# Two 16-head attentions in one Trainium2 program: two heads side by side in the row halves of TensorE

## The reference

```
# l1a, causal with a slope per head
scores = einsum('bhqd,bhkd->bhqk', q, k) * 8**-0.5
bias   = -slopes[h] * (pos[q] - pos[k])            # slopes[h] = 2**(-0.5 * (h + 1))
scores = where(pos[q] >= pos[k], scores + bias, -inf)
out    = (softmax(scores) @ v) @ Wo.T
# l3b, each block of 128 queries sees its own and the two neighbouring blocks of keys
scores = einsum('bhnqd,bhnkd->bhnqk', q, k_ctx) * 8**-0.5
scores = where(abs(q_pos - k_pos) <= 128, scores, -inf)
out    = (softmax(scores) @ v) @ Wo.T + bo
```

## Time and profile before

| what | value |
|---|---|
| median of 3 runs | 3575.45 us (3564.14 to 3583.17) |
| profiled execution, its own time | 3585.18 us |
| its span | 3583.1 us |
| PE busy over the span | 2880.5 us (80%) |
| DVE busy over the span | 1859.3 us (52%) |
| causal call: norm and projections, attention | 1195 to 1252, 1252 to 1564 us |
| windowed call: norm and projections, attention | 3189 to 3233, 3233 to 3475 us |

### The profile page before, as it was taken

How to read it: one execution, slowest core, us unless ns; L and a number is a source line. 1 busy time by engine, 2 the same in 40 slices (tenths; PEclk the granted TensorE clock), 3 DMA queues, 4 the chain that set the end, 5 groups by cost and what they waited for, 6 DMA issues and landing times. The chain is left out here.

```text
span 3583.1 us, 54951 instructions
## 1 busy us (share of the span) xinstructions
PE 2880.5 (80%) x21418; PEld 1480.1 (41%) x21486; DVE 1859.3 (52%) x3533; ACT 1405.9 (39%) x2681; POOL 765.2 (21%) x632
## 2 busy tenths in 40 slices
PE   6565878778888498989768888998888877768986
PEld 3454247423357234434322222342332434555555
DVE  5311245478964388711378888203763543536733
ACT  3211424432234246642356777422221222234652
POOL 1000006245617201000443340003530001230003
PEclk9666869878889789989879999997998989878987
DMA  2022001121101422100031010000510001023302
GB/s 109 15 63 74 0 12 45 37 72 65 53 20 51 112 44 37 21 1 0 14 70 28 12 24 1 0 0 17 145 49 0 0 1 48 20 71 62 51 6 70
DMA packets 86479, 136.40 MB, mean 38 GB/s; under 512 B 13319, under 2 KB 52199, under 8 KB 84947
## 3 DMA queue, kind: packets, MB, share of 16 engines
q1 hardware_dynamic: 79187, 118.50, 13.1%
q0 software_dynamic: 7040, 14.43, 1.5%
HBM read 106.81 MB, written 25.85 MB: 37 GB/s over the span
## 5 line engine op out<-in xcount | busy, mean ns | idle before, releaser
L1655 ACT ACTIVATE at_pt<-PS 128x384 f32<-128x384 f32 (+3 forms) x704 | 288.5, 455 | 237.7 <-PE PS L1567 202.5
L1705 DVE TENSOR_REDUCE at_mp<-PS 128x1 f32<-128x384 f32 (+3 forms) x640 | 313.5, 538 | 115.1 <-PE PS L1555 98.9
L1552 PE MATMUL PS<-at_kx,at_qx 72*128 72x384 bf16 (+5 forms) x640 | 219.0, 347 | 66.8 <-DMA at_kx<-L_attn_a_parts 26.8
L1565 PE MATMUL PS<-at_qx,at_kx 105*128 105x512 bf16 (+5 forms) x704 | 214.4, 314 | 7.8 <-ACT at_pt L1655 5.9
L4300 DVE CUSTOM_DVE_ANT_0 PS<-PS,ls_pt 128x1024 f32<-128x1024 f32 x128 | 153.8, 1237 | 19.1 <-ACT ls_pt L4153 15.5
L4153 ACT ACTIVATE ls_pt<-PS,ls_far 128x512 f32<-128x512 f32 x256 | 155.5, 686 | 18.6 <-PE PS L3974 10.1
L2425 DVE TENSOR_TENSOR_SCAN mb_ring<-PS,mb_ring 128x1024 f32<-128x1024 f32 x64 | 146.6, 2291 | 19.4 <-POOL mb_ring L2364 6.7
L2380 PE MATMUL PS<-mb_ring,ident 128*128 128x512 f32 x256 | 147.2, 728 | 6.0 <-DVE mb_ring L2430 6.0
L1227 DVE SCALAR_TENSOR_TENSOR X<-PS,small_L,X 128x512 f32<-128x512 f32 x8 | 6.0, 751 | 261.2 <-PE PS L1175 261.2
L2409 ACT ACTIVATE PS<-mb_dt,mb_a 128x1024 f32<-128x1024 f32 x64 | 71.5, 1118 | 174.8 <-DVE mb_ring L2425 169.5
L1578 PE MATMUL PS<-at_pt,at_v 128*9 128x256 f32 (+3 forms) x1408 | 130.7, 451 | 5.5 <-issue 1.4
(11 more groups left out here) (825 smaller groups left out, 6557.2 us busy)
## 6 DMA issues: line engine op xcount, KB each, us to landing
rw_arena<-rw_v_rows SPq DMA_DIRECT2D x32, 512.0 KB, 4.6
dl_arena<-in_fir_bank SPq DMA_DIRECT2D x32, 256.0 KB, 3.1
lnA<-mb_rows SPq DMA_DIRECT2D x16, 512.0 KB, 3.7
XN<-mb_rows SPq DMA_DIRECT2D x16, 512.0 KB, 3.7
ffn_place<-in_ffn_L SPq DMA_DIRECT2D x4, 1152.0 KB, 16.7
at_qx<-L_attn_a_parts SPq DMA_DIRECT2D x24, 192.0 KB
at_kx<-L_attn_a_parts SPq DMA_DIRECT2D x72, 64.0 KB
at_qx<-L_attn_b_parts SPq DMA_DIRECT2D x24, 192.0 KB
```

What stands on the lines that cost most here:

```text
L1552: mm = nc.tensor.matmul(PS[:, n % 3, 0:e - c], QX[0:RAW, u % 3, g, blk(i, P)], KX[0:RAW, u % 3, g, c:e], start=True, stop=True)
L1565: mm = nc.tensor.matmul(PS[:, 3 + n % 3, 0:e - c], KX[0:FULL, u % 3, g, blk(j, P)], QX[0:FULL, u % 3, g, c:e], start=True, stop=True)
L1655: nc.scalar.activation(PT[:, y % SLOTS, g, 0:e - c], PS[:, 3 + n % 3, 0:e - c], ACT.Exp, scale=SCALE).then_inc(exp_done, 1)
L1705: nc.vector.tensor_reduce(best, sc, AX.X, ALU.max).then_inc(s_maxed, 1)
```

## The change

- **Row halves.** A head takes 48 rows of products (six pairs of parts in place of nine), six slope rows (causal) and three rows of maxima: 57 or 51 rows. Two of the four heads stand in rows 0 to 63 (lane 0), two in rows 64 to 127 (lane 1). The first pass takes heads 0, 2, 1, 3 (lanes 0, 1, 0, 1), the second 2, 0, 3, 1 (lanes 1, 0, 1, 0), so that neighbours on PE stand in different lanes. DVE and ACT follow these orders.
- **Masks inside the halves.** `mask` adds one tile with two products of 64 rows in the head's own lane: `identb` with ABOVE, and EYE2 with OTHER (the identity and the mask of the other half). One covers 128 columns and the other 64. They are issued after both passes' products: score, turned score, score's masks, turned score's masks.
- **Loads.** 22 DMAs (causal) or 18 (windowed) per unit, with half as many elements per part; before 12 (13 for the first three units of the causal call).
- **Slopes.** POOL makes the whole slope table beside the norm, and `load` copies the rows by DMA. The work of DVE and ACT on them, L1494 and the copies of L1670 are gone, as are the two fills of 32 rows. The fixed rows of KX come from PHI, PLO and UNIT by six DMAs (windowed: two) after the stores of m = 0.
- **First load.** `load(0)` is issued after the stores of m = 3, and those of m = 4 to 7 follow it.
- `lower` sends its rows with two DMAs in place of one.

```diff
-    MROW = 102 if causal else 72
-    RAW, FULL = (102, 105) if causal else (72, 75)
...
+    LANES, SPLIT = 2, ((0, 0), (0, 1), (0, 2), (1, 0), (1, 1), (2, 0))
+    SLOPES = 6 if causal else 0
+    PLACE = 8 * len(SPLIT)
+    RAW = PLACE + SLOPES
+    FULL = RAW + 3
+    EACH = HG // LANES
+    LOADS = LANES * (9 + (EACH if causal else 0))
+    lane_rows = lambda lane, n: slice(64 * lane, 64 * lane + n)
+    head_first = lambda t: 2 * (t % 2) + t // 2
+    head_second = lambda t: 2 * (1 - t % 2) + t // 2
...
-        QX, KX = sb("at_qx", [P, 3, HG, SEQ], BF16), sb("at_kx", [P, 3, HG, SEQ], BF16)
+        QX, KX = sb("at_qx", [P, 3, HG // LANES, SEQ], BF16), sb("at_kx", [P, 3, HG // LANES, SEQ], BF16)
...
+        ABOVE, OTHER, EYE2 = sb("at_above", [P, 2, P], BF16), sb("at_other", [P, 2, P], BF16), sb("at_eye2", [P, P], BF16)
...
-            SLT = sb("at_slt", [P, 16])
-            KROWS = sb("at_krows", [P, SEQ], BF16)
...
         def load(sp, u):
-            heads, tokens = slice(HG * (u % 4), HG * (u % 4) + HG), blk(u // 4, SEQ)
-            for n in range(3):
-                rows = slice(24 * n, 24 * n + 24)
-                sp.dma_start(QX[rows, u % 3, :, :], parts[0, heads, :, :, tokens].rearrange("g c d t -> (c d) g t")).then_inc(LOADED[u % 3], 16)
-                if causal and n == 0 and u < 3:
-                    sp.dma_start(KX[72:96, u, :, :], parts[1, heads, :, :, tokens].rearrange("g c d t -> (c d) g t")).then_inc(LOADED[u], 16)
-                for c in range(3):
-                    rows = slice(24 * n + 8 * c, 24 * n + 8 * c + 8)
-                    sp.dma_start(KX[rows, u % 3, :, :], parts[1, heads, n, :, tokens].rearrange("g d t -> d g t")).then_inc(LOADED[u % 3], 16)
+            tokens = blk(u // 4, SEQ)
+            for lane in range(LANES):
+                heads = slice(HG * (u % 4) + EACH * lane, HG * (u % 4) + EACH * lane + EACH)
+                top = 64 * lane
+                for p, (c, _) in enumerate(SPLIT):
+                    sp.dma_start(QX[top + 8 * p:top + 8 * p + 8, u % 3, :, :], parts[0, heads, c, :, tokens].rearrange("g d t -> d g t")).then_inc(LOADED[u % 3], 16)
+                for at, n in ((0, 3), (24, 2), (40, 1)):
+                    sp.dma_start(KX[top + at:top + at + 8 * n, u % 3, :, :], parts[1, heads, 0:n, :, tokens].rearrange("g c d t -> (c d) g t")).then_inc(LOADED[u % 3], 16)
+                if causal:
+                    for g in range(EACH):
+                        slopes = SLT[0:SLOPES, heads.start + g, :].unsqueeze(1).to_broadcast([SLOPES, 8, SEQ // 8])
+                        sp.dma_start(QX[top + PLACE:top + RAW, u % 3, g, :].rearrange("p (r t) -> p r t", r=8), slopes).then_inc(LOADED[u % 3], 16)
...
+                own(pool.tensor_copy(EYE2[:, 0:64], k.identb[:, 64:P]))
+                own(pool.tensor_copy(EYE2[:, 64:P], k.identb[:, 0:64]))
+                for n in range(2):
+                    sign = 2 * n - 1
+                    own(pool.memset(OTHER[:, n, :], 0.0))
+                    own(pool.memset(TURN[:, :], 0.0))
+                    own(pool.affine_select(out=OTHER[:, n, :], in_=OTHER[:, n, :], compare_op=ALU.is_ge, fill=NEG, base=-64 * sign, pattern=[[sign, P]], channel_multiplier=-sign))
+                    own(pool.affine_select(out=TURN[:, :], in_=TURN[:, :], compare_op=ALU.is_ge, fill=NEG, base=64 * sign, pattern=[[sign, P]], channel_multiplier=-sign))
+                    own(pool.tensor_copy(OTHER[64:P, n, :], TURN[64:P, :]))
...
-                    own(pool.memset(QX[64:96, :, :, :], 0.0))
-                else:
...
-                    own(pool.memset(KX[64:96, :, :, :], 1.0))
+                    for n in range(3):
+                        own(pool.tensor_tensor(RM[:, n:n + 1], k.ident[:, n:n + 1], k.ident[:, n + 3:n + 4], ALU.add))
+                    own(pool.tensor_copy(SH[:, 0, :], SL[:, :]))
...
+                    for n in range(3):
+                        own(pool.tensor_scalar(SLR[:, n, :], SH[:, n, :], RM[:, n:n + 1], None, ALU.mult))
...
+                    own(pool.tensor_copy(SLT[0:SLOPES, :, :], SLR[0:SLOPES, 0, :].unsqueeze(2).to_broadcast([SLOPES, 16, SEQ // 8])))
+                own(pool.memset(UNIT[:, :], 1.0))
...
-                        if causal and m == 2:
-                            act.wait_ge(rows_known, 3)
-                            nc.scalar.activation(KROWS[96:P, :], PHI[96:P, :], ACT.Identity, scale=RM[96:P, 0:1], bias=RM[96:P, 2:3]).then_inc(rows_started, 1)
...
-                        if causal and m == 0:
-                            row_kinds()
-                        if causal and m == 3:
-                            position_rows()
...
-                if causal:
-                    @block.gpsimd
-                    def _(pool):
-                        pool.wait_ge(slopes_cut, 1)
-                        pool.wait_ge(rows_made, 1)
-                        pool.tensor_copy(QX[96:102, 0, :, :], SLT[96:102, 0:HG].unsqueeze(2).to_broadcast([6, HG, SEQ])).then_inc(first_rows, 1)
-                        pool.wait_ge(first_rows, 1)
...
-                        if m == 4:
+                        if m == 0:
+                            for lane in range(LANES):
+                                for n, rows in enumerate(KROWS):
+                                    at = 64 * lane + PLACE + 3 * n
+                                    sp.dma_start(KX[at:at + 3, :, :, :].rearrange("p s g t -> p (s g) t"), rows[0:3, :].unsqueeze(1).to_broadcast([3, 3 * EACH, SEQ])).then_inc(PLACED, 16)
+                        if m == 3:
                             for n in range(4):
                                 sp.wait_ge(STORED[n], 48)
-                            if causal:
-                                sp.wait_ge(rows_made, 1)
-                                for slot in range(3):
-                                    sp.dma_start(KX[96:105, slot, :, :], KROWS[96:105, :].unsqueeze(1).to_broadcast([9, HG, SEQ])).then_inc(PLACED, 16)
                             load(sp, 0)
...
-                            if u:
-                                pe.wait_ge(rows_ready, u)
+                    lane, g = divmod(head_first(t), EACH)
+                    if x == 0 and t == 0:
+                        pe.wait_ge(LOADED[u % 3], 16 * LOADS * (u // 3 + 1))
+                        pe.wait_ge(PLACED, 16 * LANES * (3 if causal else 1))
                     if n >= 3:
                         pe.wait_ge(s_maxed, n - 2)
-                    mm = nc.tensor.matmul(PS[:, n % 3, 0:e - c], QX[0:RAW, u % 3, g, blk(i, P)], KX[0:RAW, u % 3, g, c:e], start=True, stop=True)
-                    for j in range(c // P, e // P):
-                        if j == i if causal else j != i:
-                            mm = nc.tensor.matmul(PS[:, n % 3, j * P - c:(j + 1) * P - c], k.identb[:, :], ABOVE[:, 0 if j >= i else 1, :], start=False, stop=True, skip_group_check=True)
-                    mm.then_inc(s_ready, 1)
-
-                def score_turned(u, x, g):
-                    n = N2 * u + HG * x + g
+                    rows = lane_rows(lane, RAW)
+                    mm = nc.tensor.matmul(PS[:, n % 3, 0:e - c], QX[rows, u % 3, g, blk(i, P)], KX[rows, u % 3, g, c:e], start=True, stop=True)
+                    if not masks_first(x):
+                        mm.then_inc(s_ready, 1)
+
...
+                def mask(bank, at, kind, lane):
+                    rows = lane_rows(lane, 64)
+                    for half, eye, above in ((lane, k.identb, ABOVE), (1 - lane, EYE2, OTHER)):
+                        a, b = (64 * half, P) if kind == 0 else (0, 64 + 64 * half)
+                        mm = nc.tensor.matmul(PS[:, bank, at + a:at + b], eye[rows, :], above[rows, kind, a:b], start=False, stop=True, skip_group_check=True)
+                    return mm
+
+                def score_masks(u, x, t):
+                    n = N1 * u + HG * x + t
+                    i, c, e = first[x]
+                    for j in masks_first(x):
+                        mm = mask(n % 3, j * P - c, 0 if j >= i else 1, head_first(t) // EACH)
+                    if masks_first(x):
+                        mm.then_inc(s_ready, 1)
+
+                def score_turned(u, x, t):
+                    n = N2 * u + HG * x + t
                     h, j, c, e = second[x]
-                    if x == opens[h] and g == 0:
-                        pe.wait_ge(LOWERED[h], 16 * (u + 1))
+                    lane, g = divmod(head_second(t), EACH)
+                    if x == opens[h] and t == 0:
+                        pe.wait_ge(LOWERED[h], 16 * LANES * (u + 1))
                     if n >= 3:
                         pe.wait_ge(exp_done, n - 2)
-                    mm = nc.tensor.matmul(PS[:, 3 + n % 3, 0:e - c], KX[0:FULL, u % 3, g, blk(j, P)], QX[0:FULL, u % 3, g, c:e], start=True, stop=True)
+                    rows = lane_rows(lane, FULL)
```

(30 more changed lines are left out.)

54 lines of the change are left out of this document (21 added, 33 removed).

## The result

The median fell from 3575.2 us (3564.1 to 3583.2) to 3553.3 us (3546.1 to 3559.2): 0.9934 times the time before, 95% interval 0.9914 to 0.9953, so 22 us less. On another chip, where both kernels are about 1.2% slower, it was 0.9935 (0.9913 to 0.9957). The forecast was 3537 us with a range of 3490 to 3580: the sign held, the size was 38 us and came out at 22.

A forecast was written before the change was run, and what follows sets the result against it. PE was taken to lead in both attentions, with DVE close behind in the causal one. Causal attention 25, causal front 2.8, windowed phases 10.5, phase 0 -0.7, windowed front 0.5: 38.1 us saved, giving 3537 us, range 3490 to 3580.

The forecast's parts named there:

- The lock: Causal phases 1 to 5: a short DVE operation held until POOL's slope copy ends; removing it gains 5 x 2.6 = 13 us.
- The causal steady phase: Causal attention: longest engine per step sums to 30.2 us; four phases fall from 35.4 to 30.8 us, 18.4 us gained.
- The windowed steady phase: Windowed attention: 1.8 us gained less 0.3 for changes between halves and full array, 1.5 in each of 7 phases, 10.5 us.
- Phase 0: Windowed call, first pass alone at 1.2 GHz: 672 columns instead of 640 before the next head starts, 0.7 us lost.
- The causal end: Last causal phase, without maxima: ACT waits for the first product after the values, which is no faster, so gain 0.
- Rival E: PE granted 1.2 GHz in a third of 14 steady phases because it has less to do: 65 us, 3602 us; chance 0.06.
- The causal front: Causal call before the first product: 33.9 us from first store becomes 31.5; 2.4 us gained, 2.8 with POOL's.
- the six fixed-row DMAs: SP's queue in the causal front: copying KX's fixed rows takes 3.0 to 5.4 us.
- The windowed front: Windowed call before attention: 2.0 us from POOL and up to 2.6 from landing, less 1.8 and 2.3 for DMAs: 0.5 gained.
- C: Rival: two bf16 streams on PE don't overlap, so masks only add: 17 us slower, 3592 us; chance 0.13.
- D: Rival: a lane's weights can't load while it streams, so each mask product costs 98 ns: 93 us slower, 3668; chance 0.06.
- B: Rival: both calls fall to their floor, 27.5 us a causal and 21.5 a windowed phase, 43 us more: 3494; chance 0.10.

The follow-up runs named there:

- the fixed rows by POOL: Kernel after, with KX's fixed rows copied by DMAs that POOL issues at the start of the projections, not SP: 0.99 times the kernel before.
- the filler: Kernel after, each turned score in the causal call's phase 8 followed by a 256-column product into an unread bank: 0.9924 times the kernel before.
- the combination: Kernel after, POOL issuing fixed rows, first slope rows and third-part stores; causal masks behind the score, windowed values before the fourth head: 0.9857 times before.

## Why the prediction was right or wrong

**The lock, right and too small.** 13 us forecast, 16.3 measured. The term counted the held operation alone; PE's standing behind it also cost the clock in three of the five. The prediction had read three clocks of the attentions and saw one of 0.95 without asking why.

**The causal steady phase, right.** Step by step the longest engine gave 32.3 us without the lock and 30.2 with halves; measured 32.5 and 30.9. The forecast took 30.8.

**The windowed steady phase, one step wrong.** The same sum gave 24.1 and 23.0, a gain of 1.1, less 0.3 for the changes between halves and all rows: 0.8, as measured. The phases themselves are 1.7 and 2.0 us longer than the sums, so only their difference is confirmed. The prediction then took 1.8 "between 1.1 and 2.3", the second being PE's columns alone. That mean was the mistake: columns that PE saves in a step that DVE, ACT or a bank ends become idle time. PE's columns themselves were about right (2.3 us forecast, 2.9 less busy), masks of 64 columns included. Seven phases gave 5.9 us for 10.5. Phase 0 gave back 2.4, where a loss of 0.7 was forecast: it runs at 1.2 GHz for some 20 us, PE sets the pace there (busy 20.6 of 22 us), and a head's masks lie beside the next head's product in the other half. That the windowed attention came to 9.0 us of the 9.8 forecast is therefore luck: the phases fell short by 4.6, and phase 0 made up for 3.1.

**The causal end and the clock, missed.** For the last phase the forecast was 0; it lost 4.2 us, and two steady phases 2.2 and 1.5. Rival E had named the clock, but as a matter of a third of all phases or none, 65 us. It came in falls of 3 to 17 us, some 8 us in all. Its counter-argument, that PE had kept its clock at 3.85 of 5 us busy, was too weak: after, the clock fell behind a stretch with PE busy 4.85 of 6 us, a larger share. So the causal attention gave 17.9 us where 25 were forecast, and the falls cost about the 7 us that are missing. That less work for PE can bring such falls is shown by the windowed call without masks; what starts each of these is not shown. Of the 17.9 the halves are 1.6; without the falls it would be some 9, an estimate.

**The causal front, wrong sign.** Forecast 2.8 less, measured 3.8 more. The mis-sized term is the six fixed-row DMAs, 3.0 to 5.4 us in the prediction and 7.0 in the trace: the three for rows 64 and up took 1.4 to 1.8 us each, where the nearest row had 0.9 (nine rows of 4096 columns for three of 6144). The bounds came from a DMA of another shape. In the windowed call the one for rows 64 and up, second in line, took 0.76 us, which points to the place in the queue and not to the rows. The 24 stores took 16.7 us for 15.4; all other terms lie within their bounds or 0.2 us beside them. That they stand ahead of the stores of m = 1 to 3 and hold ACT for 9.6 us was missed too. POOL's norm part is 17.2 us for 16.7, not 0.4 less. The windowed front gave 0.2 for 0.5.

**Sum.** 7.1 us too much in the causal attention, 6.6 and 0.3 in the fronts, 0.8 in the windowed attention: 14.8, so 23.3 of 38.1. C fell by the pairs, D by the mask's 32 ns, B since a phase stays at its longest engine per step.

**So where did the change's gain come from?** Against the kernel before without POOL's copies, 632.2 us, after has 623.7: row halves, split masks, loads and the new front together are 8.5 us, of which 9.8 come from the windowed attention and 1.8 from the causal one, and 3.1 go back in the fronts. About two thirds of the result is a copy that no longer runs beside DVE (14.9 of 23.4 us in the calls, 17 of 23 by the ratios).

## What to carry to other kernels

When an engine is made faster, sum each step's longest engine and stop there; don't add a part of what the fast engine alone would give. Look first for an operation that runs 15 times its shortest time: here that was worth nearly twice all the rest (14.9 us to 8.5). And price a DMA issue by a row of its own shape and place in the queue, and ask whose buffers the stores behind it free.

## What was not expected of the hardware

- Work can be left out and the time grows: without 28 masks a head and phase, a windowed phase went from 25.0 to 27.3 us, the granted clock from 1.00 to 0.73.
- The falls of the clock come at fixed places: after shows the same two disturbed phases (33.1 and 32.2 to 32.4 us) on two chips, while the fixed rows by POOL, the filler and the combination share another pattern (32.1 to 32.2 us in the fourth).
- A change between halves and all rows costs 0.11 us each way; a mask product of 64 or 128 columns in a half 32 ns on average; a DVE stop of 2.6 us costs its phase 3.3 us on average, 3.0 to 3.8 where the clock falls behind it and 2.7 and 3.2 where it doesn't.
